# Convolution stage: a bias matmul of 128 rows, and a normalised input with one buffer per half batch

## The reference

```python
h = jnp.einsum('btd,de->bte', inputs, W1) + b1
a, g = jnp.split(h, 2, axis=-1)
x = a * jax.nn.sigmoid(g)
w = jax.nn.softmax(conv_shared_weight, axis=-1)
filt = jnp.repeat(w.T.reshape(-1), r).reshape(K, D)   # 15 taps, one filter per 16 columns
conv = lax.conv_general_dilated(x, filt, ..., padding='SAME', feature_group_count=D)
return jnp.einsum('btd,de->bte', conv, W2) + b2
```

## Time and profile before

| | |
|---|---|
| median of 3 runs | 3576.29 us (3575.45 to 3598.54) |
| profiled execution, span from first to last instruction | 3535.8 us, 40.5 below the median of the runs |
| TensorE busy | 3212.6 us (91% of the span) |
| VectorE, ScalarE, GpSimd busy | 2704.2, 2334.4, 1781.8 us |
| convolution stage, first transposes to last mixing matmul | about 2578 to 2891 us |

### The profile page before, as it was taken

One profiled execution on the slowest core, in us unless ns is written; L12 is line 12 of the kernel. 1 busy time (PEld: TensorE's weight loads), 2 busy tenths in 40 slices (PEclk: granted clock), 3 DMA queues, 4 the chain that ended last, 5 costly groups with the idle time before them and its releaser, 6 DMA issues. The chain is left out here.

```text
span 3535.8 us, 116953 instructions
## 1 busy us (share of the span) xinstructions
PE 3212.6 (91%) x46878; PEld 2155.6 (61%) x46878; DVE 2704.2 (76%) x5988; ACT 2334.4 (66%) x4989; POOL 1781.8 (50%) x3252
## 2 busy tenths in 40 slices
PE   8989899999999999999999989999779969969960
PEld 6766455555555555555555547888657656648860
DVE  7867899999999999999999954666535437855658
ACT  5555587787788777877887775777534536635533
POOL 1441377777777777777777672111000004646761
PEclk9999899999999999999999999999979989989985
DMA  7697533333333333333333312221051123336667
GB/s 242 222 261 233 90 85 84 79 81 84 82 79 82 84 81 79 83 85 79 80 84 86 75 51 93 79 90 67 25 175 48 48 73 125 116 132 184 190 203 268
DMA packets 380531, 396.76 MB, mean 112 GB/s; under 512 B 121368, under 2 KB 294424, under 8 KB 377816
## 3 DMA queue, kind: packets, MB, share of 16 engines
q1 hardware_dynamic: 366264, 351.46, 35.8%
q0 software_dynamic: 13728, 37.83, 2.9%
HBM read 230.29 MB, written 157.25 MB: 110 GB/s over the span
## 5 line engine op out<-in xcount | busy, mean ns | idle before, releaser
L809 ACT ACTIVATE att_p<-att_st 128x512 f32<-128x512 f32 (+3 forms) x3072 | 1328.4, 492 | 391.8 <-PE att_st L715 360.7
L895 DVE TENSOR_REDUCE att_mcol<-att_ring 128x1 f32<-128x512 f32 (+1 forms) x2048 | 1235.6, 650 | 125.1 <-PE att_ring L715 117.3
L715 PE MATMUL att_st<-att_ops_more 99*32 99x512 bf16 (+3 forms) x9216 | 681.2, 326 | 6.6 <-DMA att_ops_more<-att_mpart 4.8
L715 PE MATMUL att_ring<-att_ops_more 96*32 96x512 bf16 (+3 forms) x9216 | 650.8, 328 | 2.0 <-DMA att_va_more<-values 1.2
L881 POOL TENSOR_SCALAR_AFFINE_SELECT att_p<-att_p 128x512 f32<-128x512 f32 x512 | 324.2, 633 | 378.8 <-ACT att_p L809 369.9
L762 PE MATMUL att_pv<-att_p,att_va_more 128*32 128x512 f32 (+3 forms) x4608 | 475.6, 485 | 4.2 <-POOL att_p L881 2.4
L715 PEld LDWEIGHTS att_st<-att_ops_more 99*32 99x32 bf16 x9216 | 249.0, 97 | 291.5 <-ACT att_p L809 111.3
L715 PE MATMUL att_ring<-c_mask,c_identb 128*32 128x128 bf16 x8192 | 413.9, 221 | 0.0
L715 PEld LDWEIGHTS att_ring<-att_ops_more 96*32 96x32 bf16 x9216 | 252.4, 97 | 133.4 <-issue 40.4
L715 PEld LDWEIGHTS att_ring<-c_mask,c_identb 128*32 128x32 bf16 x8192 | 228.3, 98 | 82.0 <-issue 14.5
L715 PE MATMUL att_st<-att_ops 99*32 99x512 bf16 (+3 forms) x3072 | 229.4, 328 | 8.4 <-DMA att_ops<-att_mpart 8.2
(11 more groups left out here) (298 smaller groups left out, 6663.7 us busy)
## 6 DMA issues: line engine op xcount, KB each, us to landing
att_ops_more<-parts SPq DMA_DIRECT2D x1152, 64.0 KB, 3.0
parts<-prj_pt SPq DMA_DIRECT2D x128, 384.0 KB, 3.2
att_ops<-parts SPq DMA_DIRECT2D x384, 64.0 KB, 2.9
moe_work<-moe_rows SPq DMA_DIRECT2D x79, 261.0 KB
values<-prj_vs SPq DMA_DIRECT2D x16, 1024.0 KB, 6.7
heads<-att_ofin SPq DMA_DIRECT2D x128, 128.0 KB, 2.6
ffn_os<-heads SPq DMA_DIRECT2D x16, 1024.0 KB, 4.9
moe_work<-x SPq DMA_DIRECT2D x32, 512.0 KB, 4.3
```

The source lines that it names most:

```text
L715: ins = nc.tensor.matmul(out[row:row + VC], stationary[:, row:row + VC], moving, start=start, stop=stop, tile_position=(0, row))
L809: act.activation(pr[:, g % R, b, off:GN], stp[(t * NST + n) % NS][:, off:GN], ACT.Exp, scale=SCALE).then_inc(exp_done, 1)
L895: ins = v.tensor_reduce(to[:, h, c, i % HB if c else i:(i % HB if c else i) + 1], of[:, 0:w], AX.X, ALU.max)
```

## The change

The bias matmul gets 128 partitions: `inside` holds the same row pattern on all of them, and `bias_p` is cleared on all of them before its first two partitions get the bias. The three small tiles that prepare the bias move into `yb`, which isn't used until pass 0. `xn` gets a buffer for each half batch, and `norm_x` of the second half runs at tiles 6 and 7, two blocks each, in place of four at tile 8.

```diff
-        bias, bias_h, bias_t, bias_p = (m.sb(n, [2, 2 * E]) for n in ("bias", "bias_h", "bias_t", "bias_p"))
-        inside = m.sb("inside", [2, XC])
-        xs, xn = m.sb("xs", [P, XB, SB, E]), m.sb("xn", [P, GT, E])
+        bias_p, inside = m.sb("bias_p", [P, 2 * E]), m.sb("inside", [P, XC])
+        xs, xn = m.sb("xs", [P, XB, SB, E]), m.sb("xn", [P, 2, GT, E])
...
+        bias, bias_h, bias_t = (yb[0:2, 2 * n:2 * n + 2].rearrange("p t e -> p (t e)") for n in range(3))
...
-        NPAD = 2 * EC * 2 + 3
+        NPAD = 2 * EC * 2 + 4
...
-                    ins = nc.tensor.transpose(tp[k % 2][:, t * P:(t + 1) * P], xn[:, t, c * P:(c + 1) * P], C["ident"][:])
+                    ins = nc.tensor.transpose(tp[k % 2][:, t * P:(t + 1) * P], xn[:, h, t, c * P:(c + 1) * P], C["ident"][:])
...
-            def norm_x(b, h):
+            def norm_x(b, h, first, end):
                 act.wait_ge(in_scale, b + 1)
-                if b or h:
-                    act.wait_ge(x_turned, 2 * (2 * b + h))
-                for t in range(GT):
-                    ins = scaled(xn[:, t], xs[:, b % XB, h * GT + t], 0, h * GT + t)
-                ins.then_inc(xn_ready, 1)
+                if b:
+                    act.wait_ge(x_turned, 2 * (2 * b + h - 1))
+                for t in range(first, end):
+                    ins = scaled(xn[:, h, t], xs[:, b % XB, h * GT + t], 0, h * GT + t)
+                if end == GT:
+                    ins.then_inc(xn_ready, 1)
...
                     if b + 2 < B and n == 5:
-                        norm_x(b + 2, 0)
+                        norm_x(b + 2, 0, 0, GT)
...
                     if b + 2 < B and n in (6, 7):
                         round_x(b + 2, 0, n - 6)
+                        norm_x(b + 2, 1, (n - 6) * GT // 2, (n - 5) * GT // 2)
                     if 0 <= b < B and n >= 7:
                         copy_turned(b, 1, n - 7)
-                    if b + 2 < B and n == 8:
-                        norm_x(b + 2, 1)
...
             v.memset(inside[:, PAD + S:], 0.0).then_inc(pads, 1)
+            v.memset(bias_p[:], 0.0).then_inc(pads, 1)
...
+                            v.wait_ge(pads, NPAD)
+                            v.tensor_tensor(bias_p[0:2].bitcast(F32R), bias_t, bias_h, ALU.add).then_inc(bias_steps, 1)
```

More of the change, by code:

```diff
@@ L1639, in _ @@
                             act.activation(cw1h[:].bitcast(F32R), cw1[:], ACT.Copy).then_inc(w1_round, 1)
-                            act.activation(bias_h[:].bitcast(F32R), bias[:], ACT.Copy).then_inc(w1_round, 1)
+                            act.activation(bias_h.bitcast(F32R), bias, ACT.Copy).then_inc(w1_round, 1)
                     if b + 2 < B and n in (6, 7):
                         round_x(b + 2, 0, n - 6)
+                        norm_x(b + 2, 1, (n - 6) * GT // 2, (n - 5) * GT // 2)
                     if 0 <= b < B and n >= 7:
                         copy_turned(b, 1, n - 7)
-                    if b + 2 < B and n == 8:
-                        norm_x(b + 2, 1)
                 if 0 <= b < B:
@@ L1734, in _ @@
                             v.tensor_tensor(cw1l[:].bitcast(F32R), cw1[:], cw1h[:], ALU.subtract).then_inc(w1_rest, 1)
-                            v.scalar_tensor_tensor(out=bias_t[:], in0=bias_h[:], scalar=-2.0, in1=bias[:], op0=ALU.mult, op1=ALU.add)\
+                            v.scalar_tensor_tensor(out=bias_t, in0=bias_h, scalar=-2.0, in1=bias, op0=ALU.mult, op1=ALU.add)\
                                 .then_inc(bias_steps, 1)
                             v.wait_ge(bias_steps, 1)
-                            v.tensor_scalar(bias_t[:], bias_t[:], C["ident"][0:2, 1:2], None, ALU.mult).then_inc(bias_steps, 1)
+                            v.tensor_scalar(bias_t, bias_t, C["ident"][0:2, 1:2], None, ALU.mult).then_inc(bias_steps, 1)
                             v.wait_ge(bias_steps, 2)
-                            v.tensor_tensor(bias_p[:].bitcast(F32R), bias_t[:], bias_h[:], ALU.add).then_inc(bias_steps, 1)
+                            v.wait_ge(pads, NPAD)
+                            v.tensor_tensor(bias_p[0:2].bitcast(F32R), bias_t, bias_h, ALU.add).then_inc(bias_steps, 1)
                     if b >= 1 and n in (6, 7):
```

## The result

| | before | after |
|---|---|---|
| median of the runs taken together | 3580.52 us (4 runs, 3575.45 to 3598.54) | 3552.19 us (4 runs, 3546.90 to 3554.28) |
| ratio, 95% interval | | 0.992 [0.9896, 0.9943] |
| profiled execution: span | 3535.8 us | 3552.2 us (its own time is 3554.28) |

The time falls by 0.8%, some 28 us. That is within the bound of 1% and inside the range; 3544 us was forecast. The spans say the opposite, 3535.8 before and 3552.2 after, and this is the first thing to clear up: the convolution stage (first bias matmul to last mixing matmul) went from 304.7 to 271.6 us, but everything behind it from 645.5 to 701.6, though nothing there was changed.

What follows compares the result with a forecast made beforehand. TensorE was taken to set the convolution stage's length. Savings of 13 (first pass), 3.1 (pass 0), 13 (passes 1 to 5) and 3.0 (pass 6) sum to 32 us, giving 3544 us, range 3537 to 3556.

Steps and rivals of the forecast that it cites:

- the bound of 1%: Whole kernel: the time stays within 36 us, counted as not told from no change; chance 0.78.
- The price of the low matmul: Each gate tile: the two-row bias matmul costs 0.40 us at full clock, 0.57 at half, all saved by 128 rows.
- Its two terms: Loads around the bias matmul at full clock: 0.11 us lost ahead of it and 0.30 behind it.
- Passes 1 to 5: Convolution: 13 us saved, passes near 34.0 us, the wait at tile 6 growing to about 3.45, all five falling to half clock.
- Pass 0 and pass 6: Convolution: 3.1 us saved in pass 0, from eight of its nine tiles, and 3.0 in pass 6.
- First pass: Convolution's opening gate matmuls: the two-row matmul keeps the clock down; without it the pass ends 13 us earlier.
- The first rival: First pass: something other than the bias matmul keeps the clock low; 7.6 us instead of 13, about 27 in all; chance 0.13.
- From span to time: Whole kernel: the median's 40.5 us above the span carries over, so a span of about 3504 gives 3544 us.
- The slower rival: ScalarE, tiles 6 and 7: inserted 1.04 us delays sigmoid and second rounding, VectorE frees the bank later; +12 us, 3588; chance 0.03.
- The memsets: Start of the stage: hidden while VectorE waits 4.05 us for the first input; uncovered, under 1 us.

Runs made afterwards that it cites:

- buffers alone: The kernel after with the bias matmul over 2 rows as before, leaving only the two input buffers and the earlier normalising; 3589.75 us, ratio 1.0005.
- two later profiles of before: The kernel before, unedited, profiled a second and a third time; 3591.73 us (ratio 0.9991) and 3590.12 us (one run).
- 128 rows alone: The kernel after with one buffer for the normalised input and its second half normalised at tile 8 as before; 3561.95 us, ratio 0.9907.
- both halves late: The kernel after with both halves of the output's normalisation moved behind tile 8 in passes that still normalise an input; 3545.94 us, ratio 0.9865.

## Why the prediction was right, and where it was wrong

**The price of the low matmul: right.** 0.40 us a tile at full clock was forecast; steady tiles lost 0.37 to 0.40. The mechanism, two loads that come late, is what the weight-load rows show. Its two terms were off and made up for each other, which is luck: 0.11 ahead of the low matmul and 0.30 behind it were read, 0.19 and 0.21 measured. At half clock, the first tile of the first pass went from 3.58 to 3.13, which is 0.45 and not 0.57. The Trainium skill ("TensorE: Matmul & The Clock Gate", section "LDWEIGHTS (loading the stationary operand)") has a load's time follow its columns and not its rows. For the load itself the trace agrees: with the same 128 columns its median is 181, 181, 183 and 190 ns with 2, 32, 64 and 128 rows. The tile is still 0.35 to 0.40 us longer with 64 rows than with 128, because the rows decide here when the load can start; the rule, taken alone, misses that.

**Passes 1 to 5: right in mechanism, 13 forecast, 10 measured.** All five fall to half clock behind the wait, and the wait is 3.41 (3.45 forecast); a pass is 34.24 (34.0). The rest of the difference is in the kernel before: four of its five passes fell in the first profile and three in the two later ones, so it had 181.6 us to lose from and not 183.3.

**Pass 0 and pass 6: right.** Forecast 3.1 and 3.0. With the same start at full clock, pass 0 went from 33.18 (buffers alone) to 30.01; pass 6 and mixing from 52.1 to 49.3.

**First pass: the step that failed.** The text took it "that the two-row matmul keeps the clock down" and gave the first pass 13 us, against 7.6 if the clock stayed low before and after. In four later profiles with matmuls of 2 or 32 rows, and in one with 64, the clock rose 3.5 to 4.5 us after the first bias matmul. So the 35.9 us were one execution's, and in the two later profiles of before the first pass is 26.4; the change takes 5.4 from it, and another 2.1 from pass 0, which no longer begins at half clock. For the pass after the change the text had 22.9 us, and 21.0 came. The measured sum is 5.4 + 5.3 + 10.3 + 2.8 = 23.8 against 32. The first rival, 27, put nearly the right price on a wrong picture: it had the clock low on both sides, and its 7.6 us for the first pass match 5.4 + 2.1 by luck.

Why the clock rose late in two of seven profiles with a low matmul (30.5 us in the first of before, 16.8 with two low ones) and in none of six without (3.2 to 4.1 us) stays open. It is what the text proposed in a weaker form, that low matmuls make the rise less sure, but seven against six do not show it. Two more readings point the same way, on as few cases: behind the same wait of 2.43 us the clock fell in two profiles of before and not with 128 rows alone, and with two low matmuls a tile it fell behind 2.23 us in five passes of five. The Trainium skill (same page, section "What's actually happening") has sustained activity alone release the clock; the second and third profile of before agree (0.99 and 1.00 where TensorE is busy throughout), the first and the one with two low matmuls do not (0.50 at 16.70 of 16.70 us busy).

**From span to time: wrong.** The 40.5 us between the span and the median were carried over as if they lay around the execution. Each later run's time is 2.0 to 3.3 us above its own span; what made the first span short was the part behind the convolution, 645.5 us in that one execution against 709.4 and 715.9, though its convolution was 9 longer. Since this is not the change's, subtracting a gain from the median of the runs was still the right way to the time: 3576.3 - 23.8 = 3552.5, and 3552.2 was measured. That this agrees to 0.3 us is partly luck: against the runs taken beside it the time fell by 28 us (20 to 37), on another chip by 33 (27 to 39), and the stage accounts for 24. What the rest is, if it is more than scatter, stays open; the part behind the stage varied from 701.6 to 716 us over the later profiles, whatever the kernel.

**The slower rival** did not come: ScalarE still waits for TensorE ahead of both sigmoids behind the inserted activations. These tiles run at half clock in part; in the kernel with both halves late, at 1.00 throughout, ScalarE has no wait left there, and TensorE's only wait above 0.3 us in passes 1 to 5 is all the same the 0.88 us ahead of the input's transposes. ScalarE in order of time, tiles 6 to 8 of pass 2 of after:

```profile
2685.44 1.08 ACT L1578 ACTIVATE cnv_xn<-cnv_xs,cnv_nmr,cnv_rstd 128x256 f32<-128x256 f32 x2
2687.49 0.38 ACT L1601 ACTIVATE cnv_sg<-cnv_gp 128x256 f32<-128x256 f32 x1 [0.97 <-PE cnv_gp L1509]
...
2688.84 1.08 ACT L1578 ACTIVATE cnv_xn<-cnv_xs,cnv_nmr,cnv_rstd 128x256 f32<-128x256 f32 x2
2689.82 0.44 ACT L1618 ACTIVATE cnv_ct<-cnv_tp 128x342 f32<-128x342 f32 x1
2690.55 0.39 ACT L1601 ACTIVATE cnv_sg<-cnv_gp 128x256 f32<-128x256 f32 x1 [0.28 <-PE cnv_gp L1509]
```

The memsets cost nothing, as forecast. VectorE in order of time, start of the stage in after: the new memset ends 3.65 us before the first input lands.

```profile
2560.39 0.48 DVE L1714 MEMSET cnv_bias_p<- 128x512 f32 x1
2564.52 2.71 DVE L1662 BATCH_NORM_STATS2 cnv_stats<-cnv_xs 128x6 f32<-128x256 f32 x8 [3.65 <-DMA cnv_xs<-x]
```

## What to carry to other kernels

A matmul of few rows (up to 64 here) between full-height ones is dearer than its columns say, about 0.6 us in place of 0.22; where a trace shows steps longer than the neighbours' on both sides of it, pad it to the full height, or put several low ones side by side, which pay the change only once (shown here for two with the same operands). When an engine's own chain gets shorter, look at what its next wait hangs on: here work that nobody waited for stood ahead of work that TensorE waited for, and moving it took 18 us off the stage where the padding had taken 20. And a clock or a stage length read from one execution is one sample: compare the span with the times of the runs, and take a second profile before a term rests on it.

## What the runs showed of the hardware that was not expected

- The loss has a step: 2, 32 and 64 rows cost the same 0.35 to 0.40 us a tile over 128, and loads of 114 rows lose nothing. It is idle time ahead of two weight loads (0.16 and 0.24 us), whose own length stays at 181 to 190 ns. A second low matmul behind the first costs only its own 0.22 to 0.26.
- The granted clock of the same kernel in the same place was 0.50 in one execution for 30.5 us of full load and 1.00 in two others after less than 4 us.
- With 128 rows, waits of 0.88 to 1.88 us in a pass let the clock stand at 1.00, as did one of 2.43; behind every wait of 3.41 it fell. With low matmuls it fell behind 2.66 in three or four of five passes, and with two of them a tile behind 2.23 in all five. The length of the wait alone does not decide it. With the wait cut from 3.41 to 0.88 a pass became 3.88 us shorter, 1.35 more than the wait itself.
